# Layer 2's recurrence with its weights as exponentials of ramps, and its products divided anew between VectorE and GpSimd

## What is computed

```python
def wkv(w, u, k, v):
    def step(carry, kv):                      # over the 256 tokens
        aa, bb, pp = carry                    # start: 0, -inf, -inf
        kk, vv = kv
        ww = u + kk
        p = jnp.maximum(pp, ww)
        e1 = jnp.exp(pp - p)
        e2 = jnp.exp(ww - p)
        out = (e1 * aa + e2 * vv) / (e1 + e2 + EPS_WKV)     # 1e-8
        p2 = jnp.maximum(pp, kk)
        e1b = jnp.exp(pp - p2)
        e2b = jnp.exp(kk - p2)
        aa_new = e1b * aa + e2b * vv
        pp_new = p2 + jnp.log(e1b + e2b + EPS_WKV)
...
h = layer_norm(x, ln1_g, ln1_b)
k = time_shift(h, mix_k) @ Wk_t.T
v = time_shift(h, mix_v) @ Wv_t.T
r = jax.nn.sigmoid(time_shift(h, mix_r) @ Wr_t.T)
x = x + r * wkv_out
h2 = layer_norm(x, ln2_g, ln2_b)
kc = time_shift(h2, cmix_k) @ Wk_c.T
rc = jax.nn.sigmoid(time_shift(h2, cmix_r) @ Wr_c.T)
vv = jnp.square(jax.nn.relu(kc)) @ Wv_c.T
x = x + rc * vv
```

## Time and profile before

| | us |
|---|---|
| median of 3 runs | 2234.5 (2232.88 to 2235.41) |
| the profiled execution, its own time | 2244.19 |
| its span in the trace | 2242.4 |
| the stage: first scan to last statistics in it | 1194.86 to 1338.99 |

### The profile page before, as it was taken

How to read it: one execution, slowest core, us unless ns; L and a number is a source line. 1 busy time by engine, 2 the same in 40 slices (tenths; PEclk the granted TensorE clock), 3 DMA queues, 4 the chain that set the end, 5 groups by cost and what they waited for, 6 DMA issues and landing times.

```text
span 2242.4 us, 37692 instructions
## 1 busy us (share of the span) xinstructions
PE 1885.0 (84%) x13296; PEld 1250.2 (56%) x13296; DVE 1558.1 (69%) x3633; ACT 1285.2 (57%) x2737; POOL 652.3 (29%) x616
## 2 busy tenths in 40 slices
PE   7999775988999999949974288999997997589886
PEld 5777562446777777524452165566665676434465
DVE  5777685866777677458758947989997456478543
ACT  5777533776888878617755236677665212247622
POOL 3223003203544434342004532444343001221043
PEclk9999896998999999969987599999999898779898
DMA  4000004411000000035101000000000100354102
GB/s 196 1 1 2 1 1 129 138 37 38 1 1 1 1 1 1 1 90 155 58 1 77 0 1 1 1 2 1 1 1 22 36 1 1 120 164 114 57 24 78
DMA packets 80153, 87.37 MB, mean 39 GB/s; under 512 B 6578, under 2 KB 70115, under 8 KB 79073
## 3 DMA queue, kind: packets, MB, share of 16 engines
q1 hardware_dynamic: 78625, 82.49, 11.7%
q0 software_dynamic: 1344, 2.49, 0.4%
HBM read 54.39 MB, written 30.70 MB: 38 GB/s over the span
## 4 chain that ended last, share of the span: by engine, by line
PE 53%; DVE 29%; ACT 7%; issue 6%; POOL 2%; DMA 2%; SPq 0%; another core or an unknown queue 0%; DVEq 0%; ACTq 0%; POOLq 0%
PE bank L469 45%; DVE scratch L1221 5%; PE bank L653 2%; ACT XN L1996 2%; PE bank L2934 2%; PE bank L368 2%; DVE scratch L3052 1%; DVE scratch L3072 1%; PE bank L693 1%; DVE stats L245 1%; DVE XN L3092 1%; DVE scratch L1608 1%; DVE w_keep L1895 1%; ACT L2074 1%; DVE w_early L2501 1%
## 5 line engine op out<-in xcount | busy, mean ns | idle before, releaser
L469 PE MATMUL bank<-scratch 64*128 64x256 bf16 (+7 forms) x3056 | 340.2, 306 | 67.5 <-DMA scratch<-parts 39.4
L1221 DVE TENSOR_REDUCE scratch<-bank 128x2 f32<-128x512 f32 x384 | 244.6, 686 | 82.4 <-PE bank L469 79.8
L469 PEld LDWEIGHTS bank<-scratch 64*128 64x128 bf16 (+4 forms) x3056 | 184.1, 122 | 195.7 <-DVE scratch L1221 73.9
L469 PE MATMUL bank<-w_keep,scratch 128*128 128x128 f32 (+4 forms) x1760 | 245.4, 330 | 18.4 <-DVE scratch L1938 4.1
L1307 ACT ACTIVATE w_keep<-bank 128x512 f32<-128x512 f32 x384 | 212.6, 597 | 52.0 <-PE bank L469 44.3
L469 PE MATMUL bank<-XNT,w_keep 128*128 128x256 f32 (+4 forms) x800 | 238.0, 437 | 4.5 <-POOL w_keep L2135 2.2
L469 PEld LDWEIGHTS bank<-w_keep,scratch 128*128 128x128 f32 (+3 forms) x1760 | 182.7, 184 | 84.0 <-issue 55.6
L469 PEld LDWEIGHTS bank<-XNT,w_keep 128*128 128x128 f32 x800 | 149.9, 197 | 57.7 <-issue 28.4
L469 PE MATMUL bank<-w_early,scratch 64*128 64x256 f32 (+3 forms) x1152 | 164.8, 346 | 20.4 <-ACT w_early L3152 8.7
L469 PEld LDWEIGHTS bank<-w_early,scratch 64*128 64x128 f32 (+3 forms) x1152 | 120.0, 185 | 66.4 <-issue 25.6
L469 PE MATMUL bank<-w_keep 128*32 128x256 f32 (+1 forms) x1600 | 124.3, 386 | 11.3 <-ACT w_keep L1307 5.4
(11 more groups left out here) (452 smaller groups left out, 3898.7 us busy)
## 6 DMA issues: line engine op xcount, KB each, us to landing
scratch<-parts SPq DMA_DIRECT2D x24, 1024.0 KB, 5.0
parts<-scratch SPq DMA_DIRECT2D x192, 96.0 KB, 2.3
parts<-scratch SPq DMA_DIRECT2D x96, 64.0 KB, 2.1
w_early<-pack_l3f SPq DMA_DIRECT2D x1, 5206.0 KB, 14.9
w_keep<-pack_l2f SPq DMA_DIRECT2D x1, 2124.0 KB, 12.6
w_early<-pack_mamba SPq DMA_DIRECT2D x1, 2120.0 KB, 19.3
w_keep<-pack_l2x SPq DMA_DIRECT2D x1, 2049.0 KB, 7.9
w_keep<-taps SPq DMA_DIRECT2D x4, 512.0 KB, 5.3
```

Of the source, the lines that this page charges most:

```text
L469: return pe.matmul(out, lhsT, rhs, start=start, stop=stop, skip_group_check=True)
L1221: dve.tensor_reduce(neg[:, :, h], self.k.bank[5 - g % 2][:, :].rearrange("p (t s) -> p t s", s=S), AXX, ALU.max, negate=True).then_inc(*s. ...
```

## The change

The same recurrence is written with one difference for each pair of weights. With x = key minus the level before the token, the two exponents are minus the ramps: d = exp(-relu(x)), c = exp(-relu(-x)), and with u in them exp(-relu(x + u)) and exp(-relu(-x - u)). ScalarE makes both ramps and both exponentials (`ramps_act`), four activations for a pair in place of two. VectorE forms x once (`ahead_dve`) and, once the logarithm is there, x minus it (`level_dve`). GpSimd keeps two products for a part: the decayed sum (`decayed_pool`) and the value's term (`value_pool`). The weight times value, the numerator's product and sum are on VectorE. The reciprocal of the denominator becomes Ln and Exp(-1) on ScalarE, and so do the two roots of the second norm. The table with both logarithm and exponential is loaded by name, and the Sigmoid of the gates is gathered. The order in every engine's list is written anew.

```diff
@@ vector @@
+    def ahead_dve(dve, part):
...
+        dve.wait_ge(*s.stacked.at("in", part, 0))
+        scan(dve, part, pm, k3, k3, BEFORE_ALL, ALU.max, ALU.max).then_inc(*s.vector.up("p", part))
         dve.wait_ge(*s.vector.at("p", part))
-        dve.tensor_tensor(b3(d), pm[:, :, 0:S], pm[:, :, 1:PADDED], ALU.subtract).then_inc(*s.formed.up("d", part))
+        dve.tensor_tensor(b3(x), k3, pm[:, :, 0:S], ALU.subtract).then_inc(*s.formed.up("x", part))
...
-            dve.tensor_tensor(P1, P1, b3(m), ALU.add).then_inc(*s.vector.up("level", part))
...
-            dve.tensor_tensor(b3(m), P0, k3, ALU.max).then_inc(*s.formed.up("m", part))
...
-            dve.tensor_tensor(c, kk, m, ALU.subtract).then_inc(*s.formed.up("c", part))
...
+        dve.tensor_tensor(x, x, num, ALU.subtract).then_inc(*s.formed.up("x2", part))
...
-            dve.tensor_tensor(b3(m), pm[:, :, 0:S], b3(kk), ALU.max).then_inc(*s.formed.up("m2", part))
...
-            dve.tensor_tensor(c, kk, m, ALU.subtract).then_inc(*s.formed.up("c2", part))
...
+        dve.tensor_tensor(c, c, v, ALU.mult).then_inc(*s.vector.up("cv", part))
...
-            dve.reciprocal(d, d).then_inc(*s.vector.up("inverse", part))
+        dve.tensor_tensor(b3(num), b3(num), aa[:, :, 0:S], ALU.mult).then_inc(*s.vector.up("da", part))
...
+        dve.wait_ge(*s.pool.at("vc", part))
+        dve.tensor_tensor(num, num, v, ALU.add).then_inc(*s.vector.up("num", part))
+        dve.wait_ge(*s.scalar.at("inverse", part))
@@ scalar @@
+    def ramps_act(act, tag, part, x, down, up, first_bias, second_bias):
+        act.activation(down, x, ACT.Relu, bias=first_bias).then_inc(*s.lowered.up(tag, "down", part))
+        act.activation(up, x, ACT.Relu, bias=second_bias, scale=-1.0).then_inc(*s.lowered.up(tag, "up", part))
+        act.wait_ge(*s.lowered.at(tag, "down", part))
+        act.activation(down, down, ACT.Exp, scale=-1.0)
+        act.wait_ge(*s.lowered.at(tag, "up", part))
+        act.activation(up, up, ACT.Exp, scale=-1.0).then_inc(*s.weighed.up(tag, part))
+    def inverse_act(act, part):
...
+        act.wait_ge(*s.vector.at("den", part))
+        act.activation(x, x, ACT.Ln).then_inc(*s.lowered.up("den", part))
+        act.wait_ge(*s.lowered.at("den", part))
+        act.activation(x, x, ACT.Exp, scale=-1.0).then_inc(*s.scalar.up("inverse", part))
+    def log_root_act(act, tag):
+        act.wait_ge(*s.variance.at(tag))
        act.activation(k.rs[:, :], k.moments[:, 2, :], ACT.Ln, bias=k.small[:, 0:1], scale=1.0 / P).then_inc(*s.lowered.up("root", tag))
        act.wait_ge(*s.lowered.at("root", tag))
+        act.activation(k.rs[:, :], k.rs[:, :], ACT.Exp, scale=-0.5).then_inc(*s.deviation.up(tag))
@@ gpsimd @@
-        decay_pool(e, "second", FIRST)
-        value_pool(e, FIRST)
-        decay_pool(e, "third", FIRST)
-        num_pool(e, FIRST)
...
+        for part in (0, 1, 2):
+            decayed_pool(e, part)
+        decayed_pool(e, 3)
         for part in PARTS:
-            (kk, v, r, d, c, m, num), (pm, sp, aa) = streams[part]
...
+            value_pool(e, part)
@@ tensor @@
         num_pe(e, 2)
+        num_pe(e, 3)
         up_pe(e, 1)
-        num_pe(e, 3)
+        turn_half_pe(e, "later", (2, 3))
         down_pe(e, 1)
-        turn_half_pe(e, "later", (2, 3))
```

More of the change, by code:

```diff
@@ L2545, in gate_dve @@
[L2545 to L2557 removed]
+        dve.wait_ge(*s.vector.at("s", part))
@@ L2713, in act @@
         scale_act(k, e, "outer", k.X, k.XN, range(NT))
[L2714 removed]
+        e.preload_act_table_set("natural_log_exp_and_others")
+        for part in (0, 1, 2):
             input_act(e, part, 0)
[L2716 to L2720 removed]
+        weights_act(e, "first", 0)
+        input_act(e, 3, 0)
+        weights_act(e, "first", 1)
+        input_act(e, 0, 1)
@@ L2721, in act @@
+        weights_act(e, "first", 2)
+        input_act(e, 1, 1)
+        weights_act(e, "first", 3)
+        input_act(e, 2, 1)
+        input_act(e, 3, 1)
+        log_act(e, 0)
+        log_act(e, 1)
+        weights_act(e, "second", 0)
+        weights_act(e, "second", 1)
+        weights_act(e, "third", 0)
+        weights_act(e, "third", 1)
+        log_act(e, 2)
+        inverse_act(e, 0)
+        inverse_act(e, 1)
         for part in PARTS:
             input_act(e, part, 2)
-        logs_act(e, FIRST)
@@ L2724, in act @@
-        weights_act(e, "second", FIRST)
-        logs_act(e, LAST)
-        weights_act(e, "third", FIRST)
-        weights_act(e, "second", LAST)
-        weights_act(e, "third", LAST)
-        for n, tag in enumerate(("second", "later")):
-            table_act(k, e, ACT.Sqrt)
-            root_act(k, e, tag)
-            scale_act(k, e, tag, k.XN, O2, range(n * NT // 2, (n + 1) * NT // 2))
-            table_act(k, e, ACT.Sigmoid)
-            for q in (2 * n, 2 * n + 1):
-                mixed_act(e, q)
@@ L2753, in mixed_act @@
-    def mixed_act(act, q):
-        for g in range(4):
-            u = 4 * q + g
-            act.wait_ge(*s.projected.at("kc", u))
-            if q >= 2 and g == 0:
-                act.wait_ge(*s.multiplied.at("vv", q - 2))
-            act.activation(KC[q % 2][:, g * BANK:(g + 1) * BANK], k.bank[u % 2][:, :], ACT.Relu).then_inc(*s.gated.up("relu", u))
+        e.preload_act_table_set("natural_log_exp_and_others")
+        log_act(e, 3)
+        weights_act(e, "second", 2)
+        weights_act(e, "second", 3)
@@ new lines, in act @@
+        log_root_act(e, "second")
+        scale_act(k, e, "second", k.XN, O2, range(0, NT // 2))
+        weights_act(e, "third", 2)
+        weights_act(e, "third", 3)
+        relu_act(e, 0)
+        relu_act(e, 1)
+        inverse_act(e, 2)
+        relu_act(e, 2)
+        inverse_act(e, 3)
+        for u in (3, 4, 5):
+            relu_act(e, u)
+        log_root_act(e, "later")
+        scale_act(k, e, "later", k.XN, O2, range(NT // 2, NT))
+        for u in (6, 7):
+            relu_act(e, u)
@@ new lines, in act, with relu_act, receptance_act @@
+        for q in range(QUARTERS):
+            if q >= 2:
+                for u in range(4 * q, 4 * q + 4):
+                    relu_act(e, u)
+            receptance_act(e, q)
+    def relu_act(act, u):
+        q, g = divmod(u, 4)
+        act.wait_ge(*s.projected.at("kc", u))
+        if q >= 2 and g == 0:
+            act.wait_ge(*s.multiplied.at("vv", q - 2))
+        act.activation(KC[q % 2][:, g * BANK:(g + 1) * BANK], k.bank[u % 2][:, :], ACT.Relu).then_inc(*s.gated.up("relu", u))
+    def receptance_act(act, q):
```

201 lines of the change are left out of this document (88 added, 113 removed).

## The result

| | us |
|---|---|
| median before, beside the changed kernel | 2234.8 (2232.9 to 2235.4, 4 runs) |
| median after | 2197.6 (2196.4 to 2200.8, 4 runs) |
| ratio, 95% interval | 0.984 (0.982 to 0.985) |
| span of the profiled execution | 2198.7 (before 2242.4) |

The change took 37.2 us off. The forecast was 29.5, and the median lies 0.4 us under the low end of the range. In two later comparisons on the chip the same two kernels stood 30.5 and 33.0 us apart. The stage itself repeats much better than the whole, so it is what I read from here on.

The account below looks back on a forecast made before the run. VectorE's list was taken to bound the first leg, TensorE's the second. Work -14.5, collisions -18.3 and waits +2.5 gave -30.3; with +0.7 in the second leg -29.6, so 2234.5 to 2205.0 us; forecast's range 2201 to 2209, 8-in-10 range 2198 to 2213.

Parts of the forecast that it names:

- VectorE's work with its gaps, first leg: VectorE's operations from first scan to channel mixing, at unit prices: 61.2 us before, 14.5 taken off.
- collisions, first leg: VectorE slowed beside GpSimd's operations, about 1.0 us each: 21.3 us before, three collisions or 3.0 after, 18.3 off.
- first leg: From first scan to start of channel mixing, bound by VectorE's list: 85.6 us to 55.3, 30.3 less.
- second leg: The 58.5 us behind the start of channel mixing, bound by TensorE's list: +0.7 us, from -1 to +4.
- New waits: VectorE's waits in the first leg for decayed sums, fourth key, second scan and root: 5.6 against 3.1, +2.5 us.
- The tight place at the root: ScalarE's eight activations of parts 2 and 3 between level and root: 4.3 us against VectorE's 4.4, costed at 0.
- the gap of 1.00: TensorE's gap before up 2 in the second leg goes, since down 1 covers the affine: -1.0 us.
- the cover of 0.7 us: Second leg, transposes of parts 2 and 3 behind down 0: VectorE ready at about 16, TensorE at 16.7.
- A: Rival: the tail eats part through second-leg collisions, late ScalarE and dearer decayed sums; -24, about 2211 us; chance 0.20.
- B: Rival: new waits hide, squares cost TensorE nothing, collisions fall closer to none; -35, about 2200 us; chance 0.14.
- C: Rival: ScalarE bounds the first leg, deciding from 1.38 us per activation; slower, 2242 us at 1.5; chance 0.02.
- D: Rival: late ScalarE results put about 30 us of waits where collisions stood, at 1.3 to 1.4 per activation; 2234; chance 0.02.

Follow-up runs that it names:

- the reciprocal's kernel: Changed kernel with the denominators' inverse as VectorE's reciprocal again: 2211.8 us beside 2199.1 for the changed kernel, ratio to before 0.993.
- the last version: Changed kernel with all products on VectorE and part 3's raising and level moved behind the affine: 2193.4 us, ratio 0.982, stage 125.58.
- the hidden sums: Changed kernel with VectorE's sums of later parts moved ahead of raising earlier ones, hiding GpSimd's decayed sums: 2196.9 us beside 2199.7, stage 128.18.
- the last two variants: Changed kernel with decayed sums hidden behind later parts' sums, 2196.9 us; with all products on VectorE and part 3 behind the affine, 2193.4 us.

## Why the prediction came out as it did

The direction, the place and the mechanism held; the size was low by 3 us in the stage.

| term, us | forecast before → after | measured before → after |
|---|---|---|
| VectorE's work with its gaps, first leg | 61.2 → 46.7 | 58.7 → 45.1 |
| collisions, first leg | 21.3 → 3.0 | 23.8 → 2.9 |
| waits, first leg | 3.1 → 5.6 | 3.1 → 5.7 |
| first leg | 85.6 → 55.3 | 85.6 → 53.7 |
| second leg | 58.5 → 59.2 | 58.5 → 57.1 |

The measured collisions are what VectorE's slowed operations took beyond their undisturbed durations, 26 operations before and three after; the waits are its stops of 0.1 us and more, the first scan's left out; the work is the rest.

**Work and collisions.** The work taken off was 13.6 us, not 14.5, the collisions 20.9, not 18.3. The collisions had been taken as what was left of 85.6, so what the work had too much they had too little. The step that was off is the unit price of 0.70 with its gap for every operation: it is about right where one operation waits for the other (1237.26 is 0.73 behind 1236.53 after the change), but independent ones start 0.60 apart (the next at 1237.87). Before the change the 2.5 us too many in the work and the 2.5 too few in the collisions cancelled. After it the work alone was 1.6 us too high, and that is the first leg's error. The number of collisions left, three, was exact, and the three cost 2.9 us against 3.0.

The prediction called the collisions the edit's real content. They are the largest term of its sum, but the kernel with GpSimd's share on VectorE shows that removing them was worth 7.0 us of leg by itself, because VectorE then has the work. Of the 24 operations that left GpSimd with the change, 12 are on VectorE and 12, differences, have no successor in the new arithmetic, which also takes more than those 12 off VectorE's own list.

**New waits.** Forecast +2.5, measured +2.6. The three for L2818 sum to 3.8 against 3.7, the fourth key to 0.37 against 0.4, the second scan to 0.46 against 0.9, the root to 0.62 against 0.6. Four stops of 0.10 in front of the gates' products were not in the sum.

**ScalarE.** It keeps up, at a spacing of 0.52. The tight place at the root held with nothing to spare. ScalarE's last ramp set, of part 3, and the root's logarithm stand one behind the other:

```profile
1244.12 0.61 ACT L2713 ACTIVATE scratch<-scratch 128x512 f32<-128x512 f32 x1
1244.64 0.61 ACT L2715 ACTIVATE scratch<-scratch 128x512 f32<-128x512 f32 x1
1245.16 0.61 ACT L2717 ACTIVATE scratch<-scratch 128x512 f32<-128x512 f32 x1
1245.82 0.31 ACT L2743 ACTIVATE rs<-moments,small 128x16 f32<-128x16 f32 x1
```

VectorE's variance ended at 1245.78 (L258, from 1245.61, 0.17 us), the exponential at 1245.77.

**Second leg.** Forecast +0.7, measured -1.4. The squares were to cost 1.7 and cost 0.41. GpSimd's two value products and four squares were to take 1.68 each, 10.1 us; they took 1.59, 1.71, 1.49, 1.03, 1.10 and 1.43, 8.35 us, and waited 0.96 us for ScalarE's Relus between. The square of 1.03 (1258.62) ran while VectorE stood 1.66 us (to 1259.41) for the inverse of part 2, and the last two started when VectorE's operation of the moment had 0.2 and 0.5 us left. The wait was in the prediction (about 1), its effect on the squares was not; the waits for the Relus were not either. From up 1 to up 2 TensorE needed 15.45 us before (1295.79 to 1311.24) and 13.10 after: the gap of 1.00 is gone as forecast; the turning that took 1.57 us ahead of it takes 0.88 from its start to down 1's, and one of the two transposes of a part now stands ahead of up 1. Only the gap was in the sum. Both transposes of parts 2 and 3 followed down 0 without a gap, so the cover of 0.7 us was not used up.

**Rivals.** A did not come: TensorE never waits for L2560 behind down 0, though VectorE's last product there ended only 0.8 us before TensorE turned it (1266.09 and 1266.88). Its mechanism is real, since the reciprocal's kernel shows 2.67 us of just that wait. B came in part: the squares were cheap, but the decayed sums did not hide and the collisions were no fewer. With -32.6 the stage lies between forecast (-29.6) and B (-35). C and D are out by the spacing of 0.52. The range failed narrowly, by 0.4 us, in a first comparison that stood 4 to 7 us wider than the other two; the low end allowed 36.5 us, and the stage gave 32.6.

**Relu on ScalarE.** With the ramps on VectorE the stage got 7.9 us longer, so keeping them on the idle engine was right, at a little over half of the 14 us that the prediction set against it. The Trainium skill's rule ("ScalarE: Activation LUTs", Rules for kernel authors) wants relu on VectorE and gives its speed per element there for bf16. In this case's fp32 its premise holds too: a ramp takes 0.43 us on VectorE and 0.61 on ScalarE. The conclusion does not follow, since VectorE is the engine that the leg waits for.

**What stays open.** Between the first variance and the first scan the stage got 0.94 us longer (13.94 to 14.88), most of it in one group of VectorE's scalings (L351, 3.33 to 4.14). Four of its ten operations take 0.70 to 0.96 us there where undisturbed ones take 0.34, beside two operations of GpSimd of 1.56 and 1.59; before, three took 0.51 to 0.71. GpSimd's list has one operation more ahead of these (minus u, L2488, 0.23 us), so they fall elsewhere on the scalings. That is read from the rows, and no run tests it. How far the three comparisons (37.2, 30.5 and 33.0 us) differ from the stage's 32.6 by chance can't be told from these runs.

## What to carry to other kernels

Where two-input operations of VectorE and GpSimd read SBUF at the same time, moving work from the one to the other is no relief: count each move as one collision, about 1 us here, and ask whether doing it on the bounding engine is cheaper. Here it was, twice (6.9 and 3.1 us of stage), and what really freed VectorE were work left out and work given to ScalarE. The collisions of a list are best added up from its slowed operations, or shown by a kernel that removes the overlap altogether, because what is "left over" in a budget takes in the error of every unit price. And before an operation is moved out of the bounding leg, look at the next leg's queues: the last version won 3.4 us in one and lost them in the other.

## What the runs showed of the hardware

**A collision is a queue.** A product of 512 columns takes 0.69 us on VectorE alone and 1.18 on GpSimd alone. Where they meet, the rows show 1.67 and 1.68, but these are two waits and not one. GpSimd's product of 1218.82 started behind VectorE's L2532 of 1218.77: VectorE took its 0.69, GpSimd 0.50 more than alone. At 1226 the same happens with L2545, and then L2538, started while GpSimd runs, takes 0.98 more than alone and ends 0.56 behind it. So the one that starts second waits. Its own size doesn't count, as an operation of 16 columns before the change shows, which takes 0.17 undisturbed and here ends 0.04 behind GpSimd:

```profile
1272.29 1.28 POOL L2787 TENSOR_TENSOR scratch<-scratch 128x512 f32<-128x512 f32 x1
1272.37 1.24 DVE L256 TENSOR_TENSOR moments<-moments 128x16 f32<-128x16 f32 x1
```

Five such small operations make up 3.6 of the 23.8 us of collisions. GpSimd's product costs VectorE 0.98 us where VectorE's own doing costs 0.69, so its help costs 0.3 us more than no help. Scans collide as products do (2.22 for two instead of 1.27). A reciprocal, with one input, does not: 3.34 us at 1258.95 with GpSimd's squares beside it, 3.35 without. But a ramp, with one input too, does: 1.28 for 0.43.

The Trainium skill has a rule for all four ("SBUF — State Buffer", Who interferes with whom): operations with two SBUF inputs contend with GpSimd's reads, those with one do so in a two-port mode alone. These rows agree; that the ramp takes 0.43 us for 512 columns and a product 0.69 fits such a mode. That page also lets whichever issues first run and the other block fully. The rows agree there too. GpSimd's extra 0.50 at 1218.82 goes with the 0.64 that VectorE's operation still had to run, its 0.39 and 0.06 in the squares of 1261.71 and 1260.00 with 0.54 and 0.19, and VectorE's 0.98 and 1.07 (L2538, L256) with the 1.11 and 1.20 that GpSimd's had left: each time 0.13 to 0.15 less. The same holds for all 131 operations of VectorE that ran over 0.3 us longer than undisturbed beside a two-input operation of GpSimd, between 1190 and 1262 us in the fourteen traces: the excess was what was left of GpSimd's operation, less 0.12 to 0.15 us.

**TensorE's clock at the beginning of the next stage differed before and after.** The first four matrix products of the next stage took 3.75 us before and 1.95 after, for the same work:

```profile
1349.60 3.75 PE L469 MATMUL bank<-w_keep,scratch 128*128 128x512 f32 x4 [1.19 <-DVE scratch L3046]
```

```profile
1318.90 1.95 PE L469 MATMUL bank<-w_keep,scratch 128*128 128x512 f32 x4 [1.20 <-DVE scratch L3073]
```

The windows of 10.6 us right ahead of them, before and after, with the same busy times of TensorE and other granted clocks (0.53 and 0.68; 0.5 of the full 2.4 GHz is the lower level, 1.2 GHz):

```profile
1339.00:1349.60 10.60, 4.02 (x16) 3.01 (x17) 7.52 (x31) 4.45 (x10) 0.00 (x0) 0.53 0.02 3
```

```profile
1308.30:1318.90 10.60, 4.02 (x17) 3.02 (x17) 7.70 (x32) 4.46 (x10) 0.00 (x0) 0.68 0.02 3
```

The attention behind was 3.2 us shorter after the change (391.0 to 387.9), and the mixture behind that 1.9 longer (138.2 to 140.1). The change alone does not decide this. The four products took 1.95 or 1.96 us in eight of the fourteen traces, the kernel before with all products on VectorE among them, and 3.67 to 3.75 in six, among them three that were made from the changed kernel (the reciprocal, the ramps on VectorE, the hidden sums). What sets the clock there was not tried. Among the other kernels the sum of the two ran from 527.3 to 531.1 us with the same code. That is as much as the last two variants were to gain, and why the verdict on them rests on their stage.
